# A decoder layer on one core: the last batches' feed-forward matmuls placed anew between the attention stages

## The reference

```
x = layernorm(x + self_attention(x))            # causal; q and k RMS-normed and rotated
x = layernorm(x + cross_attention(x, ctx))      # causal, with a key mask
x = layernorm(x + ffn(x))
ffn(x) = W2l gelu(W1l rms(x) + b1l) + b2l       # light, 128 wide
       + W2h gelu(W1h rms(x) + b1h) + b2h       # heavy, 1024 wide; 256 of 256 tokens are
                                                # picked, so it runs on all of them
```

## Time and profile before

| what | us |
|---|---|
| median of three runs | 1015.32 |
| the profiled execution, its own time | 1012.79 |
| its span, first to last instruction | 1011.1 |
| TensorE busy in the span | 918.6 (91%) |
| VectorE busy | 734.0 (73%) |
| ScalarE busy | 489.9 (48%) |
| GpSimd busy | 468.7 (46%) |

### The profile page before, as it was taken

One profiled execution on the slowest core, in us unless ns is written; L12 is line 12 of the kernel. 1 busy time (PEld: TensorE's weight loads), 2 busy tenths in 40 slices (PEclk: granted clock), 3 DMA queues, 4 the chain that ended last, 5 costly groups with the idle time before them and its releaser, 6 DMA issues.

```text
span 1011.1 us, 21587 instructions
## 1 busy us (share of the span) xinstructions
PE 918.6 (91%) x7776; PEld 707.6 (70%) x7776; DVE 734.0 (73%) x1843; ACT 489.9 (48%) x1047; POOL 468.7 (46%) x883
## 2 busy tenths in 40 slices
PE   2577988999999999999999999999999999998896
PEld 2445565787878787777868787777878786766675
DVE  8668578787778778887777788787777788563612
ACT  1131444546364545546374655556464645445343
POOL 2264464635464554736355555636354554233221
PEclk8659899999999999999999999999999999999999
DMA  3819191917556481917456472909365462805100
GB/s 106 172 41 132 31 119 34 117 34 99 71 75 87 61 109 33 116 36 108 62 77 95 58 102 41 120 23 117 53 90 81 65 86 51 109 13 62 24 1 22
DMA packets 79643, 74.22 MB, mean 73 GB/s; under 512 B 8592, under 2 KB 78896, under 8 KB 79536
## 3 DMA queue, kind: packets, MB, share of 16 engines
q1 hardware_dynamic: 75872, 68.90, 48.9%
q10 hardware_dynamic: 3664, 3.94, 1.2%
HBM read 17.49 MB, written 4.20 MB: 21 GB/s over the span
## 4 chain that ended last, share of the span: by engine, by line
PE 63%; DVE 17%; issue 9%; POOL 5%; ACT 3%; DMA 0%; POOLq 0%; ACTq 0%; DVEq 0%
PE bank L342 58%; PE bank L367 4%; DVE mx L871 3%; POOL pr L1177 3%; ACT pr L728 2%; DVE x L948 2%; DVE y L920 1%; DVE st L927 1%; DVE rest L855 1%; DVE ss L973 1%; DVE on L911 1%; DVE nat2q L860 1%; ACT sq L817 1%; DVE nt L990 1%; DVE rden L908 1%
## 5 line engine op out<-in xcount | busy, mean ns | idle before, releaser
L728 ACT ACTIVATE pr<-bank 128x384 f32<-128x384 f32 x512 | 242.4, 499 | 209.0 <-PE bank L342 208.7
L871 DVE TENSOR_REDUCE mx<-bank 128x3 f32<-128x384 f32 x512 | 268.1, 551 | 89.0 <-PE bank L342 87.0
L1177 POOL TENSOR_SCALAR_AFFINE_SELECT pr<-pr 128x256 f32<-128x256 f32 x512 | 227.9, 453 | 215.6 <-ACT pr L728 211.4
L342 PE MATMUL bank<-w,g 128*128 128x256 f32 x576 | 170.8, 389 | 1.1 <-ACT g L740 1.1
L342 PE MATMUL bank<-cmaskb,idb 128*128 128x256 bf16 x512 | 144.5, 282 | 17.2 <-DVE mx L871 7.5
L740 ACT ACTIVATE g<-bank,b 128x256 f32<-128x256 f32 x144 | 68.3, 475 | 111.4 <-PE bank L342 110.9
L1201 POOL TENSOR_TENSOR xTlow<-xT,xThigh 128x512 fp32r<-128x512 f32 x16 | 21.2, 1322 | 173.0 <-ACT xThigh L674 173.0
L342 PEld LDWEIGHTS bank<-w,g 128*128 128x128 f32 x576 | 89.6, 190 | 5.2 <-ACT g L740 1.5
L342 PE MATMUL bank<-stk1k,stk1q 97*128 97x128 bf16 (+1 forms) x512 | 86.6, 255 | 0.0
L342 PE MATMUL bank<-stk1q,stk1k 100*128 100x256 bf16 (+1 forms) x512 | 80.6, 256 | 4.4 <-DMA stk1q<-mT 3.3
L342 PE MATMUL bank<-stk2k,stk2q 97*128 97x128 bf16 (+1 forms) x512 | 82.3, 246 | 0.0
(11 more groups left out here) (143 smaller groups left out, 1800.6 us busy)
## 6 DMA issues: line engine op xcount, KB each, us to landing
stk1q<-nat1q SPq DMA_DIRECT2D x96, 128.0 KB, 4.6
stk1k<-nat1k SPq DMA_DIRECT2D x96, 128.0 KB, 6.5
stk2k<-nat2k SPq DMA_DIRECT2D x96, 128.0 KB, 4.6
stk2q<-nat2q SPq DMA_DIRECT2D x96, 128.0 KB, 6.2
xT<-in_xT SPq DMA_DIRECT2D x16, 256.0 KB, 7.8
x<-in_x SPq DMA_DIRECT2D x16, 256.0 KB, 6.9
ctxT<-in_ctxT SPq DMA_DIRECT2D x16, 256.0 KB, 2.7
out_x<-x SPq DMA_DIRECT2D x16, 256.0 KB, 6.7
```

Of the source, the lines that this page charges most:

```text
L342: return nc.tensor.matmul(out, lhsT, rhs, start=start, stop=stop, skip_group_check=check)
L728: nc.scalar.activation(pr[:, h % (2 * HG), :], ring_bank("T", a, b, h)[:, 0:3 * P], ACT.Exp, scale=HD ** -0.5)\
L871: V.tensor_reduce(mx3[:, h, :], scored[:, 0:3 * P].rearrange("p (k t) -> p k t", k=3), AX.X, ALU.max, negate=True).then_inc(s_mx[a], 1)
L1177: G.affine_select(out=slot, in_=slot, compare_op=ALU.is_ge, fill=0.0, base=0, pattern=[[0, 2], [1, P]], channel_multiplier=-1).then_inc(s_ ...
```

## The change

In steps 16 and 17 the feed-forward calls stand elsewhere, and their waits with them. In the stage of cross scores of step 16 all nine `ffn_out(13, 0, j)` come ahead of head 0, the nine `ffn_out(13, 1, j)` take their places between heads, and `transpose_xn(14)` stands at head 14. In the next stage, which has no heads, `hidden(14, j)` follows `transpose_max(2, 15)`, and in the last transposed stage the 18 `ffn_out(14, t, j)` stand at heads 0 to 16. In step 17 nothing of batch 14 is left for TensorE; `transpose_xn(15)`, `hidden(15, j)` and `ffn_out(15, t, j)` follow the cross projection, one step earlier than before but in the same place of the queue. VectorE does layer norm 2 of batch 14 ahead of the maxima of batch 15, and the residual of batch 13 and `low_xn(14)` ahead of `max_t(2, 15)`. ScalarE does the copies and GELUs of f in steps 16 and 17, and in every step `copy_v(2, c)` ahead of the exp table load.

```diff
 def transpose_xn(b):
     pe.wait_ge(s_xn, TT * (b + 1))
-    if live(b + 1):
+    if b == B - 2:
+        pe.wait_ge(s_va[2], B)
+    elif live(b + 1):
         pe.wait_ge(s_mT[2], b + 2)
...
 # hidden, j == 1
-    if live(b + 1):
+    if b < B - 2:
         pe.wait_ge(s_oT[2], NG * (b + 2))
     else:
-        wait(pe, s_g, FCH * b)
+        pe.wait_ge(s_oT[2], NG * (b + 1))
+        pe.wait_ge(s_g, FCH * b)
...
 # transpose_max, a == 2
     pe.wait_ge(s_va[2], b + 1)
+    if b == B - 1:
+        pe.wait_ge(s_xnT, b)
...
 # values, gr == 0, a == 2
-    elif live(b - 2):
-        pe.wait_ge(s_g, FCH * (b - 1))
+    else:
+        pe.wait_ge(s_g, FCH * b)
...
 # TensorE's step; scores of s:
-if live(l):
+if live(l) and i <= B:
     for j in range(FCH):
         add(HIDDEN_AT[j], hidden, l, j)
...
 # scores of c:
-if live(l):
+if live(l) and i < B:
     for j in range(FCH):
         add(FFN0_AT[j], ffn_out, l, 0, j)
+if i == B:
+    for j in range(FCH):
+        add(0, ffn_out, l, 0, j)
+    for j in range(FCH):
+        add(FFN0_AT[j], ffn_out, l, 1, j)
+    add(14, transpose_xn, f)
...
 # transposed scores of s (transpose_xn and ffn_out(l, 1, j) only for i < B, i != B):
+if i >= B and live(f):
+    for j in range(FCH):
+        add(H, hidden, f, j)
+if i == B + 1:
+    for t in range(TT):
+        for j in range(FCH):
+            add(H, ffn_out, f, t, j)
...
 # transposed scores of c:
+if i == B:
+    for t in range(TT):
+        for j in range(FCH):
+            add((0, 8)[t] + j, ffn_out, f, t, j)
...
 # ScalarE's step
-    if live(l):
+    if live(l) and i <= B:
         gelu(l, j)
+if live(c):
+    copy_v(2, c)
+if i >= B and live(f):
+    copy_xn(f)
+    for j in range(FCH):
+        gelu(f, j)
 wait(act, s_warm, i + 2)
...
-if live(c):
-    copy_v(2, c)
...
 # VectorE's step
-if live(c):
+if i == B:
+    residual_cross()
+    statistics_cross()
+    layer_norm(2, f)
+    norm2(f)
+    scale2(f)
+    maxima(2, c, {})
+    max_parts(2, c)
+    dve.wait_ge(s_x2b, l + 1)
+    add_residual(3, l, FFN_BANK, x2b)
+    low_xn(f)
+elif live(c):
     maxima(2, c, {RESID2_AT: residual_cross, MAXT_AT: max_rows, STAT2_AT: statistics_cross})
     max_parts(2, c)
```

More of the change, by code:

```diff
@@ L635, in step @@
                     add(MAX2_AT, transpose_max, 2, c)
-                if live(f):
+                if live(f) and i != B:
                     add(XNT_AT, transpose_xn, f)
-                if live(l):
+                if live(l) and i < B:
                     for j in range(FCH):
                         add(FFN1_AT[j], ffn_out, l, 1, j)
+                if i >= B and live(f):
[5 more added lines that the diff above has]
+                            add(H, ffn_out, f, t, j)
                 if live(s):
@@ L784, in step @@
                         exponential(1, s, h)
-                    if h == COPY_XN_AT and live(f):
+                    if h == COPY_XN_AT and live(f) and i < B:
                         copy_xn(f)
@@ L1088, in step @@
                     scale_w1()
-                if live(f):
+                if live(f) and i != B:
                     low_xn(f)
                 if live(l):
-                    dve.wait_ge(s_x2b, l + 1)
-                    add_residual(3, l, FFN_BANK, x2b)
+                    if i != B:
+                        dve.wait_ge(s_x2b, l + 1)
+                        add_residual(3, l, FFN_BANK, x2b)
                     statistics(3, l)
```

## The result

The changed kernel takes 1022.25 us (median of 11 runs, 1019.77 to 1024.11) against 1015.32 (11 runs, 1013.20 to 1019.58): a ratio of 1.0062 over all runs, 95% interval 1.0048 to 1.0076, or 6.3 us more (the two medians alone lie 6.9 us apart). The forecast was 1023.0, in a range of 1018 to 1027. The profiled execution took 1023.15 us, its span is 1021.4.

The account below looks back on a forecast made before the run. The prediction took TensorE to bound the kernel. It summed +12.4 us up to the last values, -8.1 in the tail and 1.3 + 2.1 for the clock to +7.7, on 1015.3 giving 1023.0 us, range 1018.0 to 1027.0.

Parts of the forecast that it names:

- mp: Parts of batch 15's maxima, written at the end of the cross scores stage; forecast 4.6 us late, at 954.95.
- the transposes of xn: Scores stage of batch 15: four transposes come in and cost 0.66 us with what follows them.
- the stall at head 3: Scores stage of batch 15: a 0.45 us stall that the change takes away.
- Rival (2): Scores and transposed stages: fillers are free as TensorE is not the bound; -2.0 us, 1013.3 without clock loss; chance 0.06.
- To T: Up to the first transposed score of batch 15: 964.65 against 954.49, +10.2 us without clock loss.
- To V: Up to the last group of values in the transposed stage: 978.6 against 966.19, +12.4 us without clock loss.
- its 0.9 us: Transposed stage: by the skill's page on table loads, head 3 would wait and the total be 0.9 us higher.
- V to h15: Tail, last group of values to batch 15's first hidden matmul: a bare chain of 14.95 us against 23.05, -8.1.
- Before `hidden(14)`: Clock falls in the 3.4 us idle ahead of batch 14's hidden matmuls: 1.3 us, bounds 0 and 2.6.
- half of 6.8 us: Share of the time at the lower clock taken to fall on batch 14's hidden matmuls: 3.4 us, costing 1.3.
- On `hidden(15)`: Tail: clock falls in the 5.3 us gap, 4.4 us at the lower level after the first hidden matmul, costing 1.7.
- Rival (1): Clock in both emptier stretches, wait for the maxima and tail: costs nothing extra; +4.3, 1019.6 us; chance 0.19.

Follow-up runs that it names:

- e5_no_t1_fill: The changed kernel with eight of the nine `ffn_out(13, 1, j)` left out between heads of the score stage; 1019.41 us in a single execution.
- e2_half_tail: The changed kernel with the nine `ffn_out(14, 1, j)` moved from the transposed stage to behind the last cross projection; 1018.07 us, ratio to before 1.0026.
- e4_warm: The changed kernel plus 18 unread matmuls, 7 ahead of the transpose of the maxima and 11 behind the last cross projection; 1020.12 us, ratio to before 1.0043.
- e9_warm_again: The changed kernel with the same 18 unread matmuls as e4_warm, run a second time; 1020.82 us, ratio to before 1.0054.
- e3_all_tail: The changed kernel with all 18 `ffn_out(14)` in the gaps of the tail and none in the transposed stage; 1019.80 us, ratio to before 1.0037.
- e6_tail_order: The kernel before with `transpose_xn(15)` between the halves of `ffn_out(14)` and the two banks of `hidden(15, j)` in the other order; 1012.75 us, ratio 0.9974.

## Why the prediction was right

**The bound of the stages, and the price of a filler.** Forecast +4.6 to mp, measured +4.17. The main terms that stood behind it are there: 4.0 us of fillers ahead of head 0 (940.01 to 944.00), layer norm 2 under them (xn is done at 941.9), the last head near 954.5 less the offset of 2.1. Of the small terms, the transposes of xn took 0.43 and not 0.66 (heads 0.71 apart there instead of 0.28), and the stall at head 3 gave back 0.59 and not 0.45: that is the difference. The price of 0.447 us per filler is right here because the nine that come on top stand ahead of head 0, where no reduction paces TensorE. Between heads a filler is worth less: taken out, it gives back 0.25 in the score stage (e5_no_t1_fill) and 0.34 in the transposed one (e2_half_tail). Rival (2), free fillers, is refused by both.

**The wait for the maxima.** To T: forecast +10.2, and +11.5 with 1.3 for the clock; measured +11.21. The transpose waits for `low_xn`, TensorE is idle for 3.31 us (forecast 3.4), and the 9.2 us from the copy of the maxima to the first score are the projection's, not the transfer's.

**The transposed stage.** To V: +12.4, and +13.7 with the clock; measured +13.81. The stage took 14.30 us, forecast 14.0: a head and a filler every 0.65 as in the row by which it was priced, and 0.9 instead of 0.8 us for each of the three groups of values between heads. ScalarE's table load held nothing up. The Trainium skill (ScalarE: Activation LUTs, section "What ACT_TABLE_LOAD costs") adds a drain of 1.38 us to a load; in the changed kernel the load began at 967.25, 0.03 after the last GELU, ended at 968.53, and the next activation began at 968.54, so again no such drain shows, and its 0.9 us were not paid.

**The tail.** V to h15: forecast 14.95 and 0.4 for slower transposes, measured 15.49. So -7.56 where the sum has -7.7.

**The clock.** Before `hidden(14)`: forecast 1.3, measured 1.4 (e4_warm, e9_warm_again, with nothing else changed). That the size fits is in part luck: "half of 6.8 us" was a guess between 0 and 2.6, and with the same code up to T the nine chunks lost 2.4 and 2.2 us in e2_half_tail and e3_all_tail. (Six matmuls of twice 0.12 would also make 1.44 us and not the 1.3 that the working has; the traces show 1.28 for a chunk at the lower clock, so the value used was the right one.) On `hidden(15)`: forecast 1.7, measured 1.98 and 2.1 in the two profiles of the changed kernel, with 4.9 us of the chunks at the lower clock in the first where the forecast had 4.4. Rival (1), that the falls do not come, is out for the changed kernel: both came in both profiles. The Trainium skill (TensorE: Matmul & The Clock Gate, section "Part 1: The HAM clock gate") says that activity releases the lower clock; that adding activity alone takes the fall ahead of `hidden(14)` away agrees, while in the tail it did so in one of two profiles.

**The sum.** Forecast +7.7 in steps 16 to 18, profiled +8.2, timed +6.3 (4.9 to 7.7) and, the second time, +7.3 (5.4 to 9.2). The profiled difference lies above the first interval and within the second; the profiled execution of the kernel before was 2.5 us below its median, that of the changed kernel 0.9 above. A reason would be that an average execution of the kernel before loses some clock in its own thin places, as e6_tail_order's profile did (1.3 us) and the profiled one did not; this is argued from two profiles, not shown. The gap of 1.4 us between forecast and timed runs is that, or scatter.

**What I had wrong** was in the experiments. I took idle stretches to be what brings the clock down, and so expected e3_all_tail to be level with the kernel before. In the stage without fillers it fell twice with no gap over 2 us. And I expected matmuls in the large gap of the tail to be enough, where with the small ones left over the clock fell in three of four profiles (e2_half_tail, e3_all_tail and e9_warm_again, not e4_warm).

## What to carry to other kernels

Work moved out of the end of a kernel pays only down to the length of the dependent chain that it covered: here 15.2 us of matmuls (nine chunks of 0.79 and 18 products in 8.04) left a tail whose chain needed 15 of 23 us, and half of the move bought nothing. Before filling a stage, read the time from one unit of it to the next with and without a filler; a stage that looks empty because one of its partners is missing may be full already. Better is a small piece in each wait that the trace names: four chunks in the last transposed stage left its length as it was (11.12 us against 11.70, at 2.4 GHz instead of partly at 1.2) and the profile ended 4 us earlier, some of that by the order of the tail.

## What the runs showed of the hardware that I had not expected

The granted clock fell in a stage of short matmuls with gaps of only 0.6 to 2 us (e3_all_tail, at 970 and 980). In a tail that is nearly full, with 2.1 us of waiting at its end, it fell in one execution and not in another of the same kernel: `hidden(15)` took 7.69 us in e4_warm's profile and 10.20 in e9_warm_again's. Behind the same 3.31 us of idleness ahead of `hidden(14)` it was low for 3.4 us in the two profiles of the changed kernel, for 6.8 in two whose code is the same up to there (e2_half_tail, e3_all_tail), and not at all in e5_no_t1_fill, where eight fewer fillers stand in the stage ahead. The cost of such a place is thus not a number but 0 to 2.5 us by the execution, and a single profile cannot rank two kernels that differ by less.
